# Expert networks in tiles of half the array: products by pairs of experts, outputs channel-major, gates spread by DMA

## The reference

```python
# first: 8 experts, 64 -> 256 -> 64, gate = softmax of the two largest logits
h = gelu(xf @ W1[e] + b1[e]);  out += w_dense[:, e:e+1] * (h @ W2[e] + b2[e])
# second: 16 experts, 64 -> 128 -> 64
hidden = silu(x @ w1[e]) * (x @ w2[e]);  out += dispatch[:, e] * (hidden @ w3[e])
```

## Time and profile before

| | |
|---|---|
| time, median of 3 runs | 523.0 us (522.67 to 523.0) |
| profiled execution: its own time | 523.0 us |
| its span | 521.2 us |
| PE busy in the span | 464.2 us (89%) |
| DVE / ACT / POOL busy | 361.1 / 266.6 / 170.7 us |
| mean granted clock | 0.965 |
| first experts, first to last input product | 285.5 to 379.8 us |
| second experts, first to last input product | 382.6 to 510.6 us |

### The profile page before, as it was taken

How to read it: one execution, slowest core, us unless ns; L and a number is a source line. 1 busy time by engine, 2 the same in 40 slices (tenths; PEclk the granted TensorE clock), 3 DMA queues, 4 the chain that set the end, 5 groups by cost and what they waited for, 6 DMA issues and landing times.

```text
span 521.2 us, 9463 instructions
## 1 busy us (share of the span) xinstructions
PE 464.2 (89%) x3372; PEld 403.1 (77%) x3372; DVE 361.1 (69%) x1050; ACT 266.6 (51%) x631; POOL 170.7 (33%) x217
## 2 busy tenths in 40 slices
PE   0998999959239999999999999999999989989994
PEld 0687777734228898899999899999999878878893
DVE  3288778358866768978787634266477898787844
ACT  2468666521308897888897544444443223322230
POOL 4800000001312584572233324133263435434332
PEclk9999999979758999999999999999999999999997
DMA  8200000000120303000000000000000000000000
GB/s 201 95 2 1 2 1 1 0 1 1 33 48 3 80 3 82 1 3 1 2 2 1 2 0 2 1 1 0 3 1 0 1 3 0 1 14 8 2 11 10
DMA packets 5458, 8.14 MB, mean 16 GB/s; under 512 B 2850, under 2 KB 4514, under 8 KB 4900
## 3 DMA queue, kind: packets, MB, share of 16 engines
q1 hardware_dynamic: 5268, 7.43, 5.8%
q10 hardware_dynamic: 144, 0.11, 0.1%
HBM read 7.01 MB, written 0.52 MB: 14 GB/s over the span
## 4 chain that ended last, share of the span: by engine, by line
PE 69%; DVE 20%; ACT 4%; issue 4%; DMA 1%; POOL 0%; SPq 0%; DVEq 0%; ACTq 0%; POOLq 0%
PE PS L1651 10%; PE PS L1619 10%; PE PS L1636 9%; PE PS L1363 6%; PE PS L1600 6%; PE PS L1379 6%; PE PS L1524 4%; PE PS L1536 3%; PE PS L1324 2%; DVE M L934 2%; PE PS L1465 2%; PE PS L1553 2%; PE PS L1552 2%; ACT score_arena L721 2%; PE PS L1469 2%
## 5 line engine op out<-in xcount | busy, mean ns | idle before, releaser
L513 POOL TENSOR_TENSOR pr<-pr 128x512 f32<-128x512 f32 (+2 forms) x70 | 67.2, 960 | 108.6 <-DVE pr L1032 37.1
L753 ACT ACTIVATE VV<-PS 128x512 f32<-128x512 f32 x64 | 38.2, 597 | 86.8 <-PE PS L1651 86.8
L1619 PEld LDWEIGHTS PS<-wk,hid 128*128 128x128 f32 x512 | 66.6, 191 | 6.4 <-ACT hid L743 1.2
L1636 PEld LDWEIGHTS PS<-wk,hid 128*128 128x128 f32 x512 | 67.0, 191 | 5.7
L743 ACT ACTIVATE hid<-PS,wk 128x512 f32<-128x512 f32 x64 | 43.8, 687 | 49.2 <-PE PS L1600 49.2
L1619 PE MATMUL PS<-wk,hid 128*128 128x64 f32 x512 | 63.9, 268 | 0.7 <-ACT hid L743 0.7
L1636 PE MATMUL PS<-wk,hid 128*128 128x64 f32 x512 | 64.1, 268 | 0.0
L721 ACT ACTIVATE score_arena<-score_arena,nmx 128x128 f32<-128x128 f32 (+1 forms) x128 | 56.9, 447 | 13.7 <-DVE nmx L1127 13.2
L1258 DVE TENSOR_TENSOR hid<-VV,PS 128x512 f32<-128x512 f32 x64 | 43.8, 686 | 23.2 <-PE PS L1651 16.6
L1651 PE MATMUL PS<-YTs,WH 128*128 128x512 f32 x128 | 57.6, 450 | 1.8 <-DVE hid L1258 1.8
L1651 PE MATMUL PS<-YTs,WL 128*128 128x512 f32 x128 | 50.6, 395 | 0.0
(11 more groups left out here) (223 smaller groups left out, 1049.4 us busy)
## 6 DMA issues: line engine op xcount, KB each, us to landing
stage<-in_wexp SPq DMA_DIRECT2D x6, 512.0 KB, 5.9
wk<-in_w SPq DMA_DIRECT2D x1, 1032.0 KB, 8.1
wa<-in_wat SPq DMA_DIRECT2D x1, 768.0 KB, 6.3
cst<-in_consts SPq DMA_DIRECT2D x1, 580.0 KB, 6.4
X<-in_x SPq DMA_DIRECT2D x2, 256.0 KB, 5.1
out<-X SPq DMA_DIRECT2D x16, 32.0 KB, 1.9
wc<-in_w SPq DMA_DIRECT2D x2, 183.5 KB, 6.0
score_arena<-in_wcv SPq DMA_DIRECT2D x2, 144.0 KB, 6.1
```

What stands on the lines that cost most here:

```text
L513: step(nc.gpsimd.tensor_tensor(buf[:, :, 0:width], buf[:, :, 0:width], buf[:, :, width:2 * width], ALU.add))
L1619: ins = mm(accumulator(u, q, e % UNIT), hid[:, v % 3, q * P:(q + 1) * P], wk[:, W128["w2_2"]][:, r * C:(r + 1) * C], start=False, stop=(v ...
L1636: ins = mm(accumulator(u, q, e % UNIT), hid[:, v % 3, q * P:(q + 1) * P], wk[:, W128["w3"]][:, e * C:(e + 1) * C], start=True, stop=True)
```

## The change

Products are made by pairs. A tile of hidden units of each of two experts (first experts: `tile2`) is computed in one step by `split_pair`: the left expert's matmuls use array rows 0 to 63, the right one's rows 64 to 127, each with 64 rows of operands, three passes each (rounded x rounded, weight remainder x rounded, rounded x activation remainder), six matmuls of 512 columns where there were four per pair. For this a second turned copy `YX` exists with the halves swapped (fills zB, zD; `Y2` has a third block). The output product has the weights as stationary operand (64 columns) and `hid` as moving one (512 columns, float32); the left expert writes partitions 0 to 63 of a bank, the right one 64 to 127. Outputs are thus channel-major, and the gates must lie along the columns, the same on 64 partitions: the gates of a chunk are turned by PE (`gate_turn`, fills tB, tD), copied by ACT to `gate_rows`, and for each pair two DMAs of SP's queue write one row onto 64 partitions (128 KB each) in one of four buffers. `combine` is one DVE instruction of 128x512 a pair, b2 goes into it; POOL adds pairs up (`add_unit`); a matmul with `halves` adds the two halves and turns the sum back to tokens (`token_sum`, fills fC, fE). Reading out turned chunks and results in the expert stages moves from DVE to ACT, the layer norm's scaling to POOL and its rounding to ACT, and fills and steps are placed anew. The bias tiles and their preparation on POOL go. Stores stand in SP's list between gate DMAs. Beside this, PE gets three blocks of matmuls whose result nobody reads (`keep_awake`): at the start, after the convolution, and after the first turn of tokens.

```diff
+            for u in range(UNITS2 + UNITS3):
+                m, c, p = unit_of(u)
+                if p == 0:
+                    sp.wait_ge(misc_free, FILL[("tB", "tD")[m], c] + 1)
+                if u >= WIDE:
+                    sp.wait_ge(combined, u - WIDE + 1)
+                for i in range(2):
+                    sp.dma_start(gate_wide[i * C:(i + 1) * C, u % WIDE, :],
+                                 gate_rows[2 * p + i:2 * p + i + 1, c % 2, :].unsqueeze(1).to_broadcast([1, C, CW])).then_inc(gate_spread[u % WIDE], 16)
+                if u >= UNITS2 + PAIRS3 and p == STORE_AT:
+                    store(c - 1)
...
+            def combine(u):
...
+                dve.wait_ge(gate_spread[u % WIDE], 32 * (u // WIDE + 1))
...
+                    nc.vector.scalar_tensor_tensor(to, PS[:, OUT_BANKS[u % 3], :], wk[:, W128["b2"]][:, p:p + 1], gate_wide[:, u % WIDE],
+                                                   ALU.add, ALU.mult).then_inc(combined, 1)
...
+            def keep_awake(bank, times, width):
+
+                for _ in range(times):
+                    mm(PS[:, bank, 0:width], ident, cst[:, 0:width], start=True, stop=True)
...
+            keep_awake(1, 4, 2 * P)
...
+            pe.wait_ge(scaled_conv_ready, J)
+            keep_awake(2, 8, 4 * P)
...
             transpose_x(0)
+            keep_awake(2, 5, 4 * P)
...
+                for k, (w, ys) in enumerate(((WH, (YTs, YX)), (WL, (YTs, YX)), (WH, (YX, YTs)))):
+                    for i in range(2):
+                        hs = slice(i * C, (i + 1) * C)
+                        ins = mm(PS[:, banks[i], :], w[hs, m, tiles[i] * P:(tiles[i] + 1) * P], ys[i][hs, cs], start=(k == 0), stop=(k == 2))
...
+            def first_out(q):
...
+                for i in range(2):
+                    r = tile2(u, 2 * ht + i)
+                    ins = mm(PS[i * C:(i + 1) * C, OUT_BANKS[u % 3], :], wk[:, W128["w2_2"]][:, r * C:(r + 1) * C],
+                             hid[:, (2 * q + i) % 4], start=(ht == 0), stop=(ht == 1))
...
+            for q in range(2 * UNITS2):
...
+                if q >= 2:
+                    pe.wait_ge(gelu_done, 2 * q - 2)
...
+                split_pair([HID_BANKS[(2 * q + i) % 4] for i in range(2)], 0, [tile2(u, 2 * ht + i) for i in range(2)], c).then_inc(hid2_ready, 1)
+                if q >= 1:
+                    first_out(q - 1)
...
+            for r in range(UNITS3):
...
+                    elif a == 0:
+                        pe.wait_ge(silu_done, 2 * r)
+                    else:
+                        pe.wait_ge(prod3_done, 2 * r)
+                    split_pair([HID_BANKS[2 * i + a] for i in range(2)], 1 + a, [2 * p + i for i in range(2)], c).then_inc(hid3_ready, 1)
+                if r >= 1:
+                    second_out(r - 1)
```

More of the change, by code:

```diff
@@ L736, in tanh @@
                 nc.scalar.activation(PJ[:], PJ[:], ACT.Tanh).then_inc(tanh_done, 1)
[L738 to L746, removed]
+            scaled = [0]
@@ L757, in _ @@
+                if n in (29, 45, 59):
+                    output({29: 0, 45: 1, 59: 2}[n])
+            output(3)
         @block.vector
@@ L1489, in window, with token_sum @@
                 mm(PS[:, 7, n:2 * n], c_("band_prev"), wxv[:, 0], start=False, stop=True).then_inc(misc_filled, 1)
+            def token_sum(name, c):
+                late = name == "fE" and c == 3
+                if late:
+                    pe.wait_ge(acc_added, added(UNITS2 + UNITS3 - 1))
+                else:
+                    pe.wait_ge(acc_added, added(PAIRS2 * (c + 1) if name == "fC" else UNITS2 + PAIRS3 * (c + 1)))
+                take(name, c)
+                for q in range(CHUNK):
+                    ins = mm(PS[:, 7, q * C:(q + 1) * C], acc[:, c % 2, q * P:(q + 1) * P], c_("halves"), start=True, stop=not late)
+                    if late:
+                        if q == 0:
+                            pe.wait_ge(combined, UNITS2 + UNITS3)
+                        ins = mm(PS[:, 7, q * C:(q + 1) * C], weighted[:, (UNITS2 + UNITS3 - 1) % 2, q * P:(q + 1) * P], c_("halves"), start=False, stop=True)
+                ins.then_inc(misc_filled, 1)
             def result(c):
-                pe.wait_ge(fold_done, IMAGES + 8 + 4 * (c + 1))
+                pe.wait_ge(misc_free, FILL["fE", c] + 1)
                 take("oT", c)
@@ L1577, in more, with gate_turn @@
                     window(c)
+                elif kind in ("tB", "tD"):
+                    gate_turn(kind, c)
+                elif kind in ("fC", "fE"):
+                    token_sum(kind, c)
                 else:
                     result(c)
-            def accumulator(u, q, e):
-                at = (q % 2) * UNIT * C + e * C
-                return PS[:, 3 + 2 * (u % 2) + q // 2, at:at + C]
+            def gate_turn(name, c):
+                m, E = (0, E2) if name == "tB" else (1, E3)
+                pe.wait_ge(gate_ready, 4 * m + c + 1)
+                take(name, c)
+                for q in range(CHUNK):
+                    ins = mm(PS[0:E, 7, q * P:(q + 1) * P], gate[:, m, 4 * c + q, 0:E], ident, start=True, stop=True)
+                ins.then_inc(misc_filled, 1)
@@ L1587, in _, with second_out @@
+            def second_out(r):
+                u = UNITS2 + r
+                pe.wait_ge(combined, u - 2)
+                pe.wait_ge(prod3_done, 2 * r + 2)
+                for i in range(2):
+                    e = 2 * (r % PAIRS3) + i
+                    ins = mm(PS[i * C:(i + 1) * C, OUT_BANKS[u % 3], :], wk[:, W128["w3"]][:, e * C:(e + 1) * C],
+                             hid[:, (2 * r + i) % 4], start=True, stop=True)
+                ins.then_inc(out3_done, 1)
             pe.wait_ge(masked_ready, STEPS)
@@ new lines, in _ @@
+            first_out(2 * UNITS2 - 1)
+            for r in range(UNITS3):
+                c, p = divmod(r, PAIRS3)
+                if p == 0:
+                    pe.wait_ge(misc_free, FILL["zD", c] + 1)
+                for a in range(2):
+                    if r == 0:
+                        pe.wait_ge(gelu_done, 4 * UNITS2 - 1 + a)
+                    elif a == 0:
+                        pe.wait_ge(silu_done, 2 * r)
+                    else:
+                        pe.wait_ge(prod3_done, 2 * r)
+                    split_pair([HID_BANKS[2 * i + a] for i in range(2)], 1 + a, [2 * p + i for i in range(2)], c).then_inc(hid3_ready, 1)
+                if r >= 1:
+                    second_out(r - 1)
+                for what in SECOND_FILLS.get(r, ()):
+                    more(what)
```

568 lines of the change are left out of this document (320 added, 248 removed), and 6 rows, old and new, of tables (FIRST_FILLS, SECOND_FILLS).

## The result

The changed kernel takes 704.6 us (median of four runs, 703.6 to 705.2) against 523.0 us: the ratio is 1.345, with a 95% interval from 1.343 to 1.348. The forecast was 476.5 us with a range from 458 to 530. The time lies 182 us above the kernel before, on the other side of it, outside the range, and inside the band (600 to 870) of one of the rivals: the gates' source is one partition.

The account below looks back on a forecast made before the run. PE was taken to bound both expert stages, DVE the second after the change. 521.2 - 19.5 (first experts) - 24.5 (second) + 1 - 0.5 - 1.5 - 1.5 = 474.7, plus 1.8 around it: 476.5 us, range 458 to 530.

Parts of the forecast that it names:

- the gates' source is one partition: Rival: gate DMAs reading one partition get 22 GB/s, 11.7 us a unit, 861 us in all; chance 0.18.
- Gates by DMA: Spreading gates onto 64 partitions, two 128 KB DMAs a pair: at 191 GB/s a unit takes 1.4 us, hidden.
- The tiling: Expert input products: row halves run side by side, 0.70 us a pair; the rival, in sequence, 1.40, chance 0.04.
- change of tiling: PE's array switching between row and column halves: 0.15 us each, two a step, 0.30 us; bounds zero and 0.6.
- First experts: First expert stage: 32 steps of 1.86 us, fills, start wait and 6 us of stalls; 78 us instead of 97.5.
- fills at 0.4 us each: PE's fills between expert steps: about 22 in the first experts, 9 us; some 20 in the second.
- Second experts: Second expert stage: PE 92 us, DVE 96, tied in order; 106 us with slack, 24.5 less than 130.5.
- tie of PE and DVE: Second experts: PE's second input product waits for both DVE products of the pair before, some 0.3 us to spare.
- The tail: Kernel's end: shorter combine and no foldings, but a sum and turn of about 1 us; -0.5 us.
- POOL's additions: Second experts: 36 adds at 0.96 us where POOL had 48 and their foldings, so POOL gets lighter.
- the third rival: Chunks' ways longer than the cover: PE stands 15 us in the first stage, second takes 118; 490 to 512, chance 0.14.
- the forecast's own: The forecast's own band for the whole kernel's time, 464 to 490 us, chance 0.62.

Follow-up runs that it names:

- run of DMAs alone: A separate kernel with only DMAs writing 2 KB rows from different sources; 128 KB onto 64 partitions took 6.3 us from one partition, 3.0 from HBM, 2.2 from 64 partitions.
- HBM kernel: The changed kernel with each chunk's gate rows first stored to HBM and spread from there by the 96 DMAs; 502.3 us, ratio 0.956.
- the short product: Gates-through-HBM kernel with DVE's product in the second experts done for 256 of 512 columns only; 496.2 us, ratio 0.948.

## Why the prediction was wrong, step by step

**The step that failed is "Gates by DMA".** I had a row for what 64 partitions take in (191 GB/s) and none for what one partition gives, took the first as the likeliest for both, and called the transfer hidden. I had worked out the threshold, 80 GB/s. One partition gives 27, a third of it, and two experts' rows are neighbours that share it; in the kernel, where the DMAs move on to the next four partitions, it was 31 to 33. The mechanism stood among the rivals, with its condition and place, at a chance of 0.18, and outside the range. A bound that is 1/16 of the full rate at one end and all of it at the other, with no row between, does not carry 0.77 for the good end.

**The rival's price was too high**: 861 us, from 358 / 16 = 22 GB/s and 11.7 us a unit, where the units take 8.2 and 8.3 us on the mean. The slices show 33 GB/s, and at that rate the 12.6 MB of the 96 DMAs take 381 us. The run of DMAs alone had 27 for one partition and for two neighbours, but less time for partitions four apart. In the changed kernel three landings of four are 4.7 to 4.9 us apart, 27 GB/s, and the fourth, with the next group of four partitions already in the queue behind it, follows after 1.8 us: four DMAs in some 16.3 us are 32 GB/s. With two DMAs in a row from a group it was 38. That the reads of two groups overlap there fits these times; no run was made for it alone. The price that stood beside mine, about 760 us, came from the Trainium skill's 27 GB/s for one port (SBUF — State Buffer, Door 1: The DMA port swizzle); it is nearer to 704.6, and too high because it takes one port at a time for the whole stretch.

**The tiling was right.** Row halves run side by side (timeline above; 0.69 us a pair lost without it). In the HBM kernel a quiet step is short by what was forecast:

```profile
299.76 1.04 PE L1764 MATMUL PS<-cst,gate 128*8 128x128 f32 x8
300.73 0.50 PE L1773 MATMUL PS<-YTs,WH 64*128 64x512 f32 x1
...
301.62 1.08 PE L1784 MATMUL PS<-stage,wk 128*64 128x512 f32 x4
302.63 0.66 PE L1609 MATMUL PS<-cst,Y 128*128 128x128 f32 x4
303.22 0.50 PE L1773 MATMUL PS<-YTs,WH 64*128 64x512 f32 x1
```

302.63 - 300.73 = 1.90 us for a step (forecast 1.86): 0.89 for the input pair with the change of tiling in it (0.85), and 1.01 for the output (1.01).

**The rest of the sum was 26 us too low**, as the HBM kernel shows with the DMAs hidden: its span is 500.5 us, the forecast's 474.7. The parts below are worked out from starts of records.
- The experts begin at 286.4 instead of 283.4: 3 us in this trace. Seven other traces of kernels with the same program ahead of the experts have 283.6 to 285.3, so most of the 3 us is this execution. What the two more turns in attention cost was taken alone by no run.
- First experts: 87.8 us instead of 78. The two products take 62.4 (forecast 59.5), the fills 16.8 (9), idle time 8.2 (3 + 6). The failed term is "fills at 0.4 us each". In the lines above, the four transposes of L1609 take 0.59, and the gate turn of L1764, eight records, 300.73 - 299.76 = 0.97.
- Second experts: 118 us instead of 106, the upper end that I had named. The products take 87.6 (82), fills 17 (10), idle time 13 (14). A step where DVE is behind looks like this, with the wait in brackets:

```profile
397.83 0.50 PE L1773 MATMUL PS<-YTs,WH 64*128 64x512 f32 x1 [0.63 <-DVE stage L1395]
```

It is the tie of PE and DVE that was forecast, without being the main part: all such waits sum to 3.3 us, and the short product won 6.
- The tail is 0.8 us or so longer than I thought: the token sum takes 2.0 us (492.98 to 495.01), where I had about 1 for sum and turn.

```profile
492.98 0.43 PE L1656 MATMUL PS<-cst,pr 128*128 128x64 f32 x2 [0.78 <-POOL pr L572]
...
495.01 0.42 DVE L1292 TENSOR_TENSOR T<-T,PS 128x256 f32<-128x256 f32 x1 [2.08 <-PE PS L1660]
```

- `keep_awake` had its size: 3.0 us forecast, 3.4 and 3.0 us measured (505.7 - 502.3; 0.58% of 523).
- POOL's additions I priced at the 0.96 us of the earlier trace rows. That row's mean mixes three shapes; taken apart, as the lines of the kernel before are here,

```profile
L513 POOL TENSOR_TENSOR pr<-pr 128x512 f32<-128x512 f32 x31 | 40.2, 1298 | 105.5 <-DVE pr L1032 37.1 <-issue 36.4 <-DVE pr L1168 31.9
L513 POOL TENSOR_TENSOR pr<-pr 128x256 f32<-128x256 f32 x31 | 22.9, 740 | 2.4
```

the form that stays is the long one, and the HBM kernel's 39 additions take 1292 ns each:

```profile
L572 POOL TENSOR_TENSOR pr<-pr 128x512 f32<-128x512 f32 x39 | 50.4, 1292 | 97.3 <-DVE pr L1286 65.0 <-DVE pr L1283 32.2
```

It cost nothing but at the end, where the token sum waits for the last one (above, 0.78 us), since POOL is busy for 78 of 208 us in the two stages.

With the source in HBM, the time falls into the band of the third rival, the chunks' ways (490 to 512), and not into the forecast's own, but not by that rival's mechanism: PE's idle time, 8 and 13 us, is what the forecast had, and the fills are longer. So the forecast had two errors: one of mechanism, 202 us, and one of size, 26 us.

## What to carry to other kernels

A DMA has two ends. Before a broadcast is called hidden, find a row for the source as well as one for the destination: here a row that lies on one SBUF partition was read at 27 GB/s, onto 64 partitions and onto 128, and 96 such DMAs of 128 KB cost this kernel 200 us. More buffers did not help, since SP was held by issuing. Storing the rows once in HBM (16 or 32 KB a chunk) and spreading them from there took 2.9 us a DMA instead of 15.4; where that isn't possible, sources on partitions 0 to 7 and 64 to 71 brought 55 GB/s. In a profile, a DMA share of 0.8 beside 33 GB/s was the sign of it, and a median of 4.7 us for issuing a DMA another. And a sum of many small fills needs a row for each kind: "42 fills at 0.4 us" was off by 15 us.

## What the hardware showed that I had not expected

- SP's queue took in few DMAs of this kind: issuing one lasted 4.7 us, against 0.5 with an empty queue, and at most four were under way, with four buffers and with eight.
- PE takes the row halves side by side even if the program gives three matmuls of one half and then three of the other: starts 0.01 us apart, 503.9 us against 502.3. In the earlier trace rows only one product in six overlapped in such an order.
- PE's clock fell to half for 40 us in the kernel that kept PE busiest (both products on one half), and also where it waits most (0.68 in the changed kernel). The kernel before had neither in these stages, so a clock read in one version can't be carried to another.
